# Layer 0's prologue: the fourth projection behind the leading scores, two parking transfers issued by ScalarE, one product of ones

## The reference, cut to what matters

```python
xn = layernorm(x)
qs = (xn @ Wq.T).reshape(b, s, 8, 2, 16)        # 8 heads, 2 maps each
ks = (xn @ Wk.T).reshape(b, s, 8, 2, 16)
vs = (xn @ Wv.T).reshape(b, s, 8, 32)
scores = einsum('bqhif,bkhif->ibhqk', qs, ks) * 16 ** -0.5
atts = softmax(scores)
att = atts[0] - diff_weight * atts[1]
o = einsum('bhqk,bkhe->bqhe', att, vs)
```

## Time and profile before

| what | value |
| --- | --- |
| median of three runs | 1211.1 us |
| profiled execution, its own time | 1207.58 us |
| its span | 1205.5 us |
| TensorE (PE) busy | 1163.6 us, 97% |
| VectorE (DVE) busy | 901.2 us, 75% |
| ScalarE (ACT) busy | 678.4 us, 56% |
| GpSimd (POOL) busy | 570.6 us, 47% |
| granted TensorE clock, mean | 0.974 |

### The profile page before, as it was taken

One profiled execution on the slowest core, in us unless ns is written; L12 is line 12 of the kernel. 1 busy time (PEld: TensorE's weight loads), 2 busy tenths in 40 slices (PEclk: granted clock), 3 DMA queues, 4 the chain that ended last, 5 costly groups with the idle time before them and its releaser, 6 DMA issues. The chain is left out here.

```text
span 1205.5 us, 34968 instructions
## 1 busy us (share of the span) xinstructions
PE 1163.6 (97%) x14341; PEld 758.9 (63%) x14341; DVE 901.2 (75%) x1993; ACT 678.4 (56%) x1302; POOL 570.6 (47%) x599
## 2 busy tenths in 40 slices
PE   7899999999999999999989999999999999999997
PEld 6433444444444444443368797878879787888876
DVE  6777887878788787878275977777687767779675
ACT  3457676777767677667643545445344444535443
POOL 2056686777868687786622413132240414224131
PEclk8579999999999999999999999999999999999998
DMA  8515254453525444352240010010101001010100
GB/s 236 148 34 141 76 135 130 111 155 71 130 80 132 119 116 133 80 152 88 71 127 1 4 54 3 16 41 4 54 5 54 4 18 39 4 54 5 35 4 19
DMA packets 57999, 86.81 MB, mean 72 GB/s; under 512 B 8304, under 2 KB 38256, under 8 KB 57840
## 3 DMA queue, kind: packets, MB, share of 16 engines
q1 hardware_dynamic: 57840, 84.58, 26.2%
HBM read 50.40 MB, written 33.55 MB: 70 GB/s over the span
## 5 line engine op out<-in xcount | busy, mean ns | idle before, releaser
L1104 DVE TENSOR_REDUCE negmax<-s_bank 128x1 f32<-128x512 f32 x512 | 330.7, 680 | 73.5 <-PE s_bank L761 72.9
L1297 POOL TENSOR_TENSOR room<-room 128x512 f32<-128x512 f32 x248 | 310.2, 1283 | 123.0 <-ACT room L925 123.0
L925 ACT ACTIVATE room<-t_bank 128x512 f32<-128x512 f32 x512 | 283.8, 600 | 76.5 <-PE t_bank L771 73.1
L771 PE MATMUL t_bank<-qst,kst 50*128 50x512 f32 x512 | 201.9, 471 | 5.8 <-ACT room L925 5.7
L761 PE MATMUL s_bank<-kst,qst 48*128 48x512 f32 x512 | 195.4, 474 | 5.2 <-DVE negmax L1104 5.2
L771 PEld LDWEIGHTS t_bank<-qst,kst 50*128 50x128 f32 x512 | 81.8, 189 | 100.2 <-ACT room L925 63.2
L2059 POOL TENSOR_TENSOR win<-rt,apart 128x512 f32<-128x512 f32 x32 | 42.0, 1333 | 210.1 <-DVE rt L1865 210.1
L1589 PE MATMUL pr<-xt_h,win_h 128*128 128x512 f32 x256 | 106.1, 414 | 0.0
L2046 POOL TENSOR_TENSOR ex<-ex,rc 128x256 f32<-128x256 f32 x64 | 41.8, 654 | 130.2 <-DVE rc L1893 130.1
L1589 PE MATMUL pr<-xt_h,win_l 128*128 128x512 f32 x256 | 100.5, 392 | 0.0
L1589 PE MATMUL pr<-xt_l,win_h 128*128 128x512 f32 x256 | 100.2, 391 | 0.0
(11 more groups left out here) (325 smaller groups left out, 2581.7 us busy)
## 6 DMA issues: line engine op xcount, KB each, us to landing
park<-qk_h SPq DMA_DIRECT2D x128, 128.0 KB, 2.5
qst<-park SPq DMA_DIRECT2D x64, 192.0 KB, 3.2
kst<-park SPq DMA_DIRECT2D x64, 192.0 KB, 4.1
park<-qk_l SPq DMA_DIRECT2D x64, 128.0 KB, 2.4
room<-in_x SPq DMA_DIRECT2D x8, 512.0 KB, 5.0
xr<-in_x SPq DMA_DIRECT2D x8, 512.0 KB, 5.9
room<-x SPq DMA_DIRECT2D x8, 512.0 KB, 3.9
out<-so SPq DMA_DIRECT2D x32, 128.0 KB, 1.7
```

The lines of the kernel that those rows point to most:

```text
L771: pe.matmul(t_bank[w % 2][:, :], kst[slot][rows, j, c * P:(c + 1) * P], qst[slot][rows, j, :], start=True, stop=True).then_inc(m.t_done, 1)
L925: act.activation(probs[:, c, j, :], t_bank[w % 2][:, :], ACT.Exp, scale=SCALE0).then_inc(m.exp_done, 1)
L1104: dve.tensor_reduce(negmax[:, i_par, 2 * odd + j, c:c + 1], s_bank[n % S_BANKS][:, :], X, ALU.max, negate=True).then_inc(m.max_done, 1)
L1297: add = pool.tensor_tensor(sums[:, pair, h, :], probs[:, 2 * pair, h, :], probs[:, 2 * pair + 1, h, :], ALU.add)
```

## The change

Four things are changed in layer 0's prologue. (1) BETA's eight products become one of 128 columns. (2) Of PROJ 0's parking, the two transfers of the k side are issued by ScalarE, behind its copy of PROJ 0; SyncE issues the other two of qk_h and both of qk_l. (3) TensorE does PROJ 3 behind all 22 leading scores and into a_bank instead of misc, and waits for the copies of gk and beta behind it. (4) PROJ 3's copy on ScalarE goes into the first batch, behind the exponential of step (0, 4); its qk_l on VectorE to step (0, 6) and the low waves to step (0, 8). The first value step, which writes a_bank, waits for that qk_l.

```diff
-        first_banks = (a_bank, d_bank, misc, t_bank[0], t_bank[1], a_bank, d_bank, t_bank[1], misc)
+        first_banks = (a_bank, d_bank, misc, t_bank[0], t_bank[1], a_bank, d_bank, t_bank[1], a_bank)
...
-                for side, r in ((0, 0), (0, 1), (1, 0), (1, 2)):
+                for side, r in ((0, 0), (0, 1), (1, 0), (1, 2))[:4 if i else 2]:
...
                     pe.wait_ge(shared.kdb_ok, HP)
-                    for hp in range(HP):
-                        mm = pe.matmul(bank[:, KC * P + 2 * NREL * hp:KC * P + 2 * NREL * (hp + 1)], shared.ones[:, :],
-                                       shared.kdb[:, hp, :], start=True, stop=True)
-                    mm.then_inc(shared.g_psum, 1)
+                    pe.matmul(bank[:, KC * P:KC * P + 2 * NREL * HP], shared.ones[:, :],
+                              shared.kdb[:, :, :].rearrange("p h r -> p (h r)"), start=True, stop=True).then_inc(shared.g_psum, 1)
...
                 if c == 0:
                     wait(pe, m.a_evac, y)
+                if isinstance(b, int) and (b, hf, c) == (0, 0, 0):
+                    pe.wait_ge(m.qk_low, 4)
...
                 if n == UNITS:
                     first_job(len(FIRST_JOBS) - 2)
-                    pe.wait_ge(shared.g_ok, 2)
-                    first_job(len(FIRST_JOBS) - 1)
+            first_job(len(FIRST_JOBS) - 1)
+            pe.wait_ge(shared.g_ok, 2)
             for n in range(len(FIRST_JOBS) - 1):
                 pe.wait_ge(*done(n))
             pe.wait_ge(m.fold, 5)
-            prev = FIRST_JOBS[-1]
+            prev = FIRST_JOBS[-2]
...
-            for n, (kind, i, k) in enumerate(FIRST_JOBS):
+            for n, (kind, i, k) in enumerate(FIRST_JOBS[:-1]):
                 side(kind, i, k, first_banks[n])
+                if (kind, i) == ("PROJ", 0):
+                    act.wait_ge(m.qk_high, 1)
+                    for side_, r in ((1, 0), (1, 2)):
+                        act.dma_start(park[0, side_, :, r, :, :].rearrange("o r q -> r o q"),
+                                      qk_h[P // 2 * side_:P // 2 * (side_ + 1), :].bitcast(F32)).then_inc(m.parked[side_], 16)
...
                         if (hf, w) == GATE_EXP:
                             side("GEXP", b, 0)
+                        if first and (hf, w) == (0, 4):
+                            side(*FIRST_JOBS[-1], first_banks[-1])
...
-            side("PROJ", 3, 0, first_banks[8])
-            shared.low_waves(dve)
...
                         for step in range(len(GATE)):
                             if GATE[step] == (hf, w):
                                 gate(b, step)
+                        if first and (hf, w) == (0, 6):
+                            side(*FIRST_JOBS[-1], first_banks[-1])
+                        if first and (hf, w) == (0, 8):
+                            shared.low_waves(dve)
```

## The result

| | before | after |
|---|---|---|
| median of 7 runs each, us | 1211.10 (1206.74 to 1215.96) | 1204.71 (1200.22 to 1207.30) |
| ratio, 95% interval | | 0.9936 (0.9912 to 0.9960) |
| profiled execution, its span | 1207.58, 1205.5 | 1206.24, 1204.5 |
| mean granted clock in it | 0.974 | 0.975 |

The change gains 6.4 us, more than twice the 2.8 of the forecast (1208.3), though 1204.7 lies inside its range. The profiled executions differ by 1.3 us only: that of after is among its slowest, that of before among its fastest. So one trace of each can't say where 6.4 us went, and more of both were taken (E3, E13 to E16).

The account below looks back on a forecast made before the run. TensorE, busy for 97% of the span, was taken as the bound, with time lost ahead of 50 us. Terms -0.75 - 2.9 + 1.1 + 0 - 0.25 = -2.8 us gave a median of 1208.3, range 1203.5 to 1213.

Parts of the forecast that it names:

- the shifts: Start of the kernel, ahead of the first batch: gains of 0.75 us from parking and 2.9 from moving projection 3.
- The parking term: Front: two parking issues moved to ScalarE bring the first score 0.75 us earlier, between 0 and 1.24.
- Projection 3: Moved behind the leading scores on TensorE, its late work no longer delaying maximum 22: 2.9 us gained, ends 2.3 and 3.3.
- The product of ones: Ahead of the first score: one product taking 0.6 us instead of sixteen small matmuls in 3.57; by itself worth nothing.
- what comes back: First batch: the moved copy, qk_l and waves delay TensorE again by 1.1 us together, ends 0.3 and 2.4.
- SyncE's queue: Later parking 3 and fills stand ahead of half 1's placed maxima; no wait taken, bound 1 us.
- the 5.8 of the rival: Half 1's placed maxima land late at half transfer rate: wait of 5.8 us, kernel 3.0 slower; chance 0.1.
- the clock: First batch: rise behind the same value step changes nothing; 0.25 us gained taken, ends 1.45 each way.
- its rival: Clock rises earlier, behind projection 3 or the first value step: 1.45 to 2.9 us more gained; chance 0.2.
- the lasting rise: First batch, behind the second value step: the clock back at 1.00 at 67 to 68 us.
- Same: Whole kernel: a change within 6.1 us, about 0.5%, holding the forecast and the three rivals that keep its sign.
- the early clock: Clock rising behind projection 3 or the first value step: total gain 4.3 to 5.7 us, about 1206; chance 0.2.

Follow-up runs that it names:

- E3: The changed kernel again, unedited, for the clock of each run; 1204.45 us over 10 runs, ratio 0.9939.
- E13: The kernel before, unedited, one more profiled execution to see where TensorE's clock is low; 1210.84 us.
- E16: The changed kernel, unedited, one more profiled execution; 1203.86 us.
- E11: E10's order with projection 3 done directly behind projection 2, ahead of the small products, which go to a score bank; 1203.07 us, ratio 0.9928.
- E8: The changed kernel without ScalarE's parkings, keeping the product of ones and projection 3's move; 1206.33 us, ratio 0.9950.
- E6: The changed kernel with SyncE's load of x behind the placing of half 1's maxima; one execution, 1199.91 us.
- E10: E6's kernel again, timed: the changed kernel with the load of x behind the placed maxima; 1202.89 us, ratio 0.9928.
- E1: The kernel before with the product of ones and ScalarE's two parkings alone, projection 3 not moved; 1209.89 us, ratio 0.9979.
- E7: The changed kernel with projection 3's copy, its qk_l and the low waves back in front of the first batch; 1209.98 us, ratio 0.9968.
- E12: The kernel before with ScalarE's two parkings alone; one execution, 1211.43 us, beside a before of 1217.11.
- E2: The changed kernel with before's parkings and small products, so projection 3's move alone; 1210.67 us, ratio 0.9981.
- E4: The changed kernel plus dense matmuls of ones with unread results, ahead of and between scores, to keep the clock; 1227.55 us, ratio 1.0127.
- E5: The changed kernel with the value product of step (0, 1) done right behind projection 3; 1205.59 us, ratio 0.9940.

## Why the prediction was right and wrong

**Right: the shifts.** The parking term was 0.75 and measured 0.7: from parking to first score it takes 11.00 to 11.07 us in the three traces of before and 10.20 to 10.43 in the four of after. That is more than half of the 1.24 us of issues taken from SyncE. Where the rest went isn't shown. A long issue moved from the q fill, whose two take 1.62 in the earlier trace rows and 0.82 now, to the k fill, 0.89 before and 1.90 now; but in E11 the k fill takes 0.89, and the first score is no sooner, 10.26 us behind its first parking at 17.28:

```profile
22.37 0.89 SPq L567 DMA_DIRECT2D kst<-park  x2
...
27.54 1.22 PE L761 MATMUL s_bank<-kst,qst 48*128 48x512 f32 x3 [1.48 <-DMA kst<-park]
```

The Trainium skill's page "DMA: Bandwidth & Descriptors", section "Issuing engines are not separate DMA queues", has only the time on the sequencer saved; the trace agrees, and here that was a fifth of what the shifts gave (0.7 of 3.55). Projection 3 was worth 2.9 and measured 2.85. The product of ones costs 0.78, within its ends of 0.44 and 0.94, and brings the first score nothing alone (E8).

**Nearly right: what comes back.** Predicted 1.1 by ScalarE's and VectorE's late work and none in SyncE's queue. Measured 0.6 at the transposes and 0.2 before the second value step, and 0.45 at half 1's first exponential score, where the text said that a wait would be wrong. It lies within the bound of 1 named for it, far below the 5.8 of the rival. E6 and E10 show its cause: with the maxima ahead of the load of x it is gone.

**Wrong: the clock.** The step that failed is the one that reads "if the rise comes behind the same value step, nothing changes; I take 0.25 gained", together with the 0.2 given to its rival. The rise behind projection 3 comes in three of four traces of after, and M0 to M1 is then 2.9 us shorter, the upper price of that rival. The argument against it was that TensorE was busy 0.93 of 50 to 60 us and the clock stayed at 0.50. That row mixes scores with two value products, each six matmuls of 280 columns in some 1.6 us, and says nothing of six matmuls of 512 columns in 2.8 us; and it comes from one execution. Three other kernels with before's wait behind projection 3 (E1, E7, E12) show the rise in their one trace each; there the 3 us of idle time used it up, and E7 differs from after only in the place of three pieces of work. With these moved, TensorE works through a stretch of full clock that it otherwise spends waiting. None of the three traces of before has the stretch, though, and why after has it more often isn't shown; ScalarE's parkings are a rival to the moved projection there. By the Trainium skill's "TensorE: Matmul & The Clock Gate", Part 1, the full clock comes for sustained activity. The traces agree in so far as the rise stands right behind six matmuls in a row; the first trace of after has the same order of matmuls as the other three and no early rise, so the order alone doesn't decide it.

The text also had the lasting rise at 67 to 68 us. It came at 71.25 in the first trace, 4.1 us behind the second value step's end instead of about 1. M1 to M2 got 1.8 us longer in the mean for 1.25 of waits, and the later place of the rise in the order is the likely rest, which no run tests.

**Missing: the low stretch near 100 us.** In two of three traces of before, and in E1, E2, E4 and E7, the clock falls 3.3 to 4.1 us behind M3 for 7 to 10 us, and M3 to M4 takes 18.8 to 20.5 instead of 16.4. None of four traces of after has it, nor E5, E6, E8 to E11; nor has E12, though, nor before's first, and E4 and E7 have it with nearly all of the change in them. So it isn't shown that the change keeps it away, and a third of the sum above hangs on that. The prediction read its durations from that one trace of before, which lacks it. Nothing in the instructions there was changed; what decides it is open.

**The chances.** "Same" had 0.8 with a limit of 6.1 us, and 0.15 was left for more. The error is that the executions' spread was taken as noise, when about two thirds of its variance goes with the mean clock, which a change can move. The mean clock of before's 60 runs beside the experiments is 0.967 to 0.977, of after's up to 0.983; within before, each us spent at the low clock goes with some 0.44 us of time. The range's lower end doesn't follow from its terms either: the early clock's 5.7 with 0.49 more for a full parking gain gives 1204.9 and not 1203.5, so that the measured 1204.7 lies inside the range by luck.

## What to carry to other kernels

Where the granted clock differs from one execution to the next, take several traces of before and write down every rise and fall: the worth of a step is then a distribution. Ask of each idle time of TensorE whether a stretch of full clock runs out in it; filling it can be worth more than its own length. And when transfers are issued sooner, measure where the first consumer starts: here 1.24 us fewer in front of the fills were 0.7 there.

## What was not expected of the hardware

- The early rise comes in some executions of one program and not in others: M0 to M1 was 18.15 in one trace of after and 15.24 to 15.50 in three.
- Full-width matmuls between scores of 48 rows did not raise the clock in 31 us without a gap (E4: 0.50 from 25.5 to 63.0), and each pair lost 2 x (0.72 - 0.45) = 0.54 us to the alternation, an estimate from the two distances.
- Time outside the span was 2.1 us in before, E2 and E8 and 1.8 in the seven timed kernels whose ScalarE issues transfers (after with E3, E1, E4, E5, E7, E10, E11). The cause wasn't sought.
- Two issues on ScalarE took 1.25 us, as long as two on SyncE: moving an issue divides the queue and makes no issue cheaper.
